# Local attention of the last two layers: another order of rotation, squares and value copies, and a GpSimd that adds all rotated products

## The reference, cut to what matters

```
h = shift_token(x);  q, k, v = split(h @ wqkv, 3)          # 8 heads of 64
q = l2norm(q) * qs;  k = l2norm(k) * ksc
q = q*cos*scale + rotate_half(q)*sin*scale                 # k: the same, divided by scale
sim = q*8 @ k.T   in windows of 64, own and previous window, causal mask
o = softmax(sim) @ v;  x = x + o @ wo
h = layernorm(shift_token(x));  a, g = split(h @ w1 + b1, 2)
x = x + (a * gelu(g)) @ w2 + b2
```

## Time and profile before

| | |
|---|---|
| median of 3 runs | 1512.34 us (1511.67 to 1512.66) |
| profiled execution | 1508.53 us, span 1506.5 us |
| mean granted TensorE clock | 0.957 |
| busy share of the span: PE, DVE, ACT, POOL | 89%, 67%, 53%, 24% |
| the last two layers | from 1078 us to the end of the span |

### The profile page before, as it was taken

The page is one execution under the profiler, slowest core; times in us unless marked ns, Lnnn a source line. Parts: engine busy times, 40 slices in busy tenths (PEclk is TensorE's granted clock), DMA queues, the critical chain, the costliest instruction groups (busy, mean ns, idle before and its releaser), DMA issues.

```text
span 1506.5 us, 23829 instructions
## 1 busy us (share of the span) xinstructions
PE 1333.5 (89%) x9009; PEld 790.8 (52%) x9009; DVE 1013.3 (67%) x2202; ACT 792.7 (53%) x1681; POOL 361.6 (24%) x288
## 2 busy tenths in 40 slices
PE   6999999999999999999589999987279988799886
PEld 4767677776777673333223333333146654366652
DVE  5767767687766856765577667740967775877755
ACT  4544435444444442434136666675169984499851
POOL 0000000011000003335410000000267771477732
PEclk9999999999999999999569999999589999999998
DMA  5000000000000000002023111100200000000000
GB/s 141 1 1 1 1 1 1 1 1 1 1 1 1 0 1 1 1 0 81 29 77 82 46 37 37 36 3 7 57 1 2 2 2 1 1 2 2 2 1 28
DMA packets 23725, 26.03 MB, mean 17 GB/s; under 512 B 5602, under 2 KB 20140, under 8 KB 22316
## 3 DMA queue, kind: packets, MB, share of 16 engines
q1 hardware_dynamic: 23612, 24.51, 5.5%
HBM read 20.11 MB, written 4.39 MB: 16 GB/s over the span
## 4 chain that ended last, share of the span: by engine, by line
PE 64%; ACT 14%; DVE 13%; issue 4%; POOL 2%; DMA 2%; SPq 0%; POOLq 0%; DVEq 0%; ACTq 0%
PE ps L679 13%; PE ps L699 8%; PE ps L714 7%; ACT probsT L2283 6%; PE ps L1051 4%; PE ps L1010 4%; PE ps L1031 3%; DVE negmax L1437 2%; PE ps L888 2%; PE ps L882 2%; PE ps L1182 2%; PE ps L650 2%; ACT v_st L2253 2%; PE ps L1173 2%; PE ps L872 2%
## 5 line engine op out<-in xcount | busy, mean ns | idle before, releaser
L2208 ACT ACTIVATE probsT<-ps 128x512 f32<-128x512 f32 (+1 forms) x304 | 163.6, 576 | 103.7 <-PE ps L1035 91.6
L1437 DVE TENSOR_REDUCE negmax<-ps 128x1 f32<-128x1024 f32 x128 | 150.7, 1219 | 72.5 <-PE ps L699 72.4
L2030 ACT ACTIVATE probs<-ps,negmax 128x1024 f32<-128x1024 f32 x128 | 142.5, 1114 | 80.5 <-DVE negmax L1437 76.5
L2036 ACT COPY probsT<-ps 128x512 f32<-128x512 f32 x128 | 74.8, 584 | 168.2 <-PE ps L714 168.1
L714 PEld LDWEIGHTS ps<-ident,probs 128*128 128x128 f32 x1024 | 114.5, 141 | 66.2 <-issue 44.0
L714 PE MATMUL ps<-ident,probs 128*128 128x128 f32 x1024 | 138.4, 277 | 6.6 <-DVE probsT L1450 3.4
L2360 POOL TENSOR_SCALAR rstd<-mv 128x4 f32<-128x4 f32 (+1 forms) x23 | 5.3, 233 | 578.5 <-DVE mv L1372 578.4
L1010 PE MATMUL ps<-arena 76*128 76x512 bf16 (+3 forms) x384 | 113.6, 355 | 26.4 <-DVE cmax L1705 20.6
L699 PE MATMUL ps<-k_st,q_st 64*128 64x512 f32 x512 | 128.7, 622 | 5.9 <-ACT probs L2030 5.9
L1705 DVE CUSTOM_DVE_ANT_0 k_st<-ps,rel 128x256 f32<-128x256 f32 (+7 forms) x128 | 96.8, 756 | 44.1 <-PE ps L1010 43.2
L1705 DVE CUSTOM_DVE_ANT_0 q_st<-ps,rel 128x256 f32<-128x256 f32 (+7 forms) x128 | 96.7, 756 | 41.9 <-PE ps L1010 41.0
(11 more groups left out here) (245 smaller groups left out, 2565.1 us busy)
## 6 DMA issues: line engine op xcount, KB each, us to landing
arena<-c_parts SPq DMA_DIRECT2D x32, 192.0 KB
arena<-c_parts SPq DMA_DIRECT2D x16, 128.0 KB
arena<-in_L_ffn_w_dram SPq DMA_DIRECT2D x3, 512.0 KB
c_parts<-probsT SPq DMA_DIRECT2D x2, 768.0 KB, 3.5
arena<-in_c_far_dram SPq DMA_DIRECT2D x16, 96.0 KB
c_parts<-work SPq DMA_DIRECT2D x2, 768.0 KB, 11.3
work<-in_L_ffn_wqkv_dram SPq DMA_DIRECT2D x1, 1536.0 KB
x_sb<-in_L_attn_x_dram SPq DMA_DIRECT2D x2, 512.0 KB, 5.9
```

The lines of the kernel that those rows point to most:

```text
L1437: dve.tensor_reduce(negmax[:, u:u + 1], s2, AX_X, ALU.max, negate=True).then_inc(s_a_negmax, 1)
L2030: act.activation(probs[:, u % NPB, :], s2, ACT.Exp, bias=negmax[:, u:u + 1], accum_out=rowsum[:, u:u + 1]).then_inc(s_a_exp, 1)
L2208: act.activation(c_p[:, kt % 2, j0:j0 + heads, q0 - kt * P:q0 - kt * P + n], ps[:, 4 + c % 2, 0:heads * n].rearrange("p (h n) -> p h n", n ...
```

## The change

In both layers: `rotate` no longer waits for the square but for the projection, and the square waits for the rotation. On VectorE the rotation moves from the start of step t (for tile t+2) to the end of step t (for tile t+3), with the inverse of the row sums between its two products; the norms go behind the residual; the copy of 64 rows of values is done there instead of on ScalarE. On ScalarE the square goes from the end of a step to behind the value copies. On GpSimd one addition of 1024 columns (`add_halves`) takes the place of the two halves, at the end of a step and a tile further ahead.

```diff
@@ VectorE
-                    dve.wait_ge(s_d_sq, n + 1)
+                    dve.wait_ge(s_d_qkp, n + 1)
                     if exists(t, -2):
                         dve.wait_ge(s_d_add, n - 1)
                     dve.tensor_tensor(mA, qk, heads(rot_c[:, t:t + 1, :, :]), ALU.mult)
+                    if between:
+                        between()
...
-            def add_keys(l, t):
-                    n, par = TILES * l + t, t % 2
-                    dve.wait_ge(s_d_m, n + 1)
-                    dve.tensor_tensor(d_kq[par][:, INNER:2 * INNER], d_mA[:, par, INNER:2 * INNER],
-                                      d_mB[:, par, INNER:2 * INNER], ALU.add).then_inc(s_d_addk, 1)
...
             def step(l, t, piece=None):
-                    if exists(t, 2):
-                        rotate(l, t + 2)
+                    def inverse():
+                        dve.wait_ge(s_d_e, n + 1)
+                        dve.reciprocal(d_rr[:, par, :], d_sum[:, par, :]).then_inc(s_d_rr, 1)
...
-                    if exists(t, 2):
-                        add_keys(l, t + 2)
-                        norms(l, t + 2)
                     if exists(t, -2):
                         dve.wait_ge(s_d_w, n - 1)
                         z = xT[:, (t - 2) * P:(t - 1) * P]
                         dve.tensor_tensor(z, ps[:, 3, 0:P], z, ALU.add).then_inc(s_d_z, 1)
+                    if exists(t, 2):
+                        norms(l, t + 2)
                     if piece:
                         piece()
+                    if exists(t, 3):
+                        rotate(l, t + 3, inverse)
+                    elif exists(t, 0):
+                        inverse()
                     if exists(t, 0):
-                        dve.wait_ge(s_d_e, n + 1)
-                        dve.reciprocal(d_rr[:, par, :], d_sum[:, par, :]).then_inc(s_d_rr, 1)
+                        if exists(t, -1):
+                            dve.wait_ge(s_d_v, n)
+                            if exists(t, -2):
+                                dve.wait_ge(s_d_o, n - 1)
+                            dve.tensor_copy(d_vs[WIN:P, par, :], d_va[WIN:P, 1 - par, :]).then_inc(s_d_vs, 1)
+                        else:
+                            dve.sem_inc(s_d_vs, 1)
@@ ScalarE
-                    act.wait_ge(s_d_qkp, n + 1)
+                    act.wait_ge(s_d_m, n + 1)
...
+                        act.wait_ge(s_d_vp, n + 1)
                         if exists(t, -1):
-                            act.wait_ge(s_d_v, n)
-                            act.copy(d_vs[WIN:P, par, :], d_va[WIN:P, 1 - par, :])
-                        act.wait_ge(s_d_vp, n + 1)
+                            act.wait_ge(s_d_vs, n)
                         act.copy(d_va[:, par, :], ps[:, 3, :])
                         act.copy(d_vs[0:WIN, par, :], ps[0:WIN, 3, :]).then_inc(s_d_v, 1)
+                    if exists(t, 2):
+                        square(l, t + 2)
...
-                    if exists(t, 3):
-                        square(l, t + 3)
@@ GpSimd
+            def add_halves(l, t):
+                    pool.wait_ge(s_d_m, n + 1)
+                    if exists(t, -2):
+                        pool.wait_ge(s_d_qkt, n - 1)
+                    pool.tensor_tensor(kq, d_mA[:, par, :], d_mB[:, par, :], ALU.add).then_inc(s_d_add, 1)
...
                     if exists(t, 2):
                         unit_norm(l, t + 2)
+                    if exists(t, 3):
+                        add_halves(l, t + 3)
@@ TensorE, before the product with the values
+                        if exists(t, -2):
+                            pe.wait_ge(s_d_vs, n)
```

More of the change, by code:

```diff
@@ L423, in build @@
         s_d_v = sem("s_d_v")
-        s_d_addk = sem("s_d_addk")
+        s_d_vs = sem("s_d_vs")
         s_d_s = sem("s_d_s")
@@ L1765, in tables, with rotate @@
                                                   sc[:, n:n + 1, e:e + 32].to_broadcast([P, QT, 32]), ALU.mult))
-            def rotate(l, t):
+            def rotate(l, t, between=None):
                     n, par = TILES * l + t, t % 2
@@ L1784, in rotate @@
                     ins.then_inc(s_d_m, 1)
[L1786 to L1790 removed]
             def norms(l, t):
                     n, par = TILES * l + t, t % 2
+                    dve.wait_ge(s_d_sq, n + 1)
                     dve.tensor_reduce(ss[:, par, :], d_sq[:, par, :].rearrange("p (h d) -> p h d", d=HD2),
@@ L1884, in _ @@
             rotate(0, 0)
-            add_keys(0, 0)
             norms(0, 0)
             rotate(0, 1)
-            add_keys(0, 1)
             norms(0, 1)
+            rotate(0, 2)
             for l in range(DEPTH):
@@ L1936, in _ @@
                     last_norm(0)
-                else:
-                    add_keys(l + 1, 0)
-                    norms(l + 1, 0)
                 gated(l, 10)
                 if not last:
+                    norms(l + 1, 0)
                     next_shift(l, 1)
@@ L1955, in _ @@
                     add_down(l, 3)
-                    add_keys(l + 1, 1)
                     norms(l + 1, 1)
                     next_shift(l, 2)
+                    rotate(l + 1, 2)
                     next_shift(l, 3)
@@ L2309, in _ @@
                 if l == 0:
-                    for t in range(3):
+                    for t in range(2):
                         square(l, t)
@@ L2330, in _ @@
                     if l + 1 < DEPTH:
-                        if j == 8:
+                        if j == 9:
                             square(l + 1, 0)
@@ L2335, in _ @@
                     act.activation(tpre[:, 1:2], eps_c[:, 0:1], ACT.Exp)
-                    square(l + 1, 2)
         @block.gpsimd
@@ L2478, in _ @@
             pool.wait_ge(s_d_init, 1)
-            def unit_norm(l, t):
+            def add_halves(l, t):
                     n, par = TILES * l + t, t % 2
@@ L2496, in step, with begin @@
                     n, par = TILES * l + t, t % 2
-                    if exists(t, 0):
-                        v = d_p[:, par, :, :]
-                        pool.wait_ge(s_d_rr, n + 1)
-                        pool.tensor_tensor(v, v, d_rr[:, par, :].unsqueeze(2).to_broadcast([P, H2, P]), ALU.mult)\
-                            .then_inc(s_d_p, 1)
+                    v = d_p[:, par, :, :]
+                    pool.wait_ge(s_d_rr, n + 1)
+                    pool.tensor_tensor(v, v, d_rr[:, par, :].unsqueeze(2).to_broadcast([P, H2, P]), ALU.mult)\
+                        .then_inc(s_d_p, 1)
                     if exists(t, 2):
                         unit_norm(l, t + 2)
-            unit_norm(0, 0)
-            unit_norm(0, 1)
+                    if exists(t, 3):
+                        add_halves(l, t + 3)
+            def begin(l):
+                add_halves(l, 0)
+                unit_norm(l, 0)
+                add_halves(l, 1)
+                unit_norm(l, 1)
+                add_halves(l, 2)
+            begin(0)
             for l in range(DEPTH):
@@ L2515, in _ @@
                 if l + 1 < DEPTH:
-                    unit_norm(l + 1, 0)
-                    unit_norm(l + 1, 1)
+                    begin(l + 1)
             for c in range(NCH):
```

8 lines of the change are left out of this document (4 added, 4 removed).

## The result

The changed kernel takes 1522.01 us (median of 4 runs, 1521.3 to 1522.66) against 1512.45 of the kernel before (4 runs, 1511.67 to 1512.66): +9.6 us, ratio 1.007, 95% interval 1.0057 to 1.0082. The forecast was 1522, with 1507 to 1526 as range. The profiled execution took 1521.85 us, its span is 1519.8 (before 1508.53 and 1506.5).

What follows compares the result with a forecast made beforehand. The prediction took a 9.04 us TensorE-ScalarE loop as the bound, replaced by a clamp-held loop of 9.42. Terms 7.6 + 5.6 - 3.6 + 1.1 - 1.3 = +9.4 on 1508.53, plus 3.8 to the median, gave 1522 us (range 1507 to 1526).

Steps and rivals of the forecast that it cites:

- the loop: TensorE and ScalarE chain of a steady step, 9.04 us; without the square 8.14, but a second loop of TensorE allows 8.77.
- the clamp is held: Steady steps: VectorE's clamp waits nearly 2.1 us for GpSimd's addition; step 9.04 to 9.42, +7.6 us over both layers.
- One sign of the forecast: In the profile after, ScalarE should stand idle over 1 us a step waiting for the transposes of q and k.
- the terms above: Forecast parts: steady steps +7.6, step 13 +5.6, layer starts -3.6, first layer's start +1.1, between layers -1.3; sum +9.4 us.
- The locked loop: Steady steps: addition, clamp, product, inverse, multiplication, power, scaling, and addition again, closing at 9.42 us; forecast's chance 0.50.
- the bounds: Limits for GpSimd's addition of 1024 columns: 2.13 us, from an earlier stage's operation, to 2.56, twice the half.
- the addition is always first: Steady steps: addition starts 4.0 after the multiplication, clamp 4.03 to 4.14, so the addition leads by 0.03 to 0.14 us.
- the clamp gets in ahead of the addition: Rival, chance 0.15: order turns, steady steps of some 8.8 and 9.2 alternate, mean about 9.04; 1514 to 1517 us.
- Step 13: Clamp ahead of the shift released 2.0 later, step 12's shift (0.84) in the loop: +2.8 per layer, +5.6 us.
- The first steps: First two steps of each layer are free of the clamp's loop and lose the square: 4 x 0.90 = -3.6 us.
- Step 14: No long addition against the clamp in steps 14 and 15; missing ScalarE copy and waiting copy about cancel: 0.
- The third rotation ahead of the tables: Layer start: it leaves the first maxima's path (2.4), but the third addition holds the tables as long: 0 (-2.3 to +1).

Runs made afterwards that it cites:

- copy on ScalarE: Changed kernel with the copy of the 64 rows of values back on ScalarE, in front of its own tile's values: 1516.49 us, ratio 1.0035.
- second profile: The same changed kernel measured and profiled once more, nothing edited: 1522.95 us, ratio 1.0078 to the kernel before.
- no clamp: Changed kernel without VectorE's clamp of the 16 sums of squares; the power takes the sums as they are: 1511.40 us, ratio 1.0001.
- two additions: Changed kernel with GpSimd's addition of 1024 columns cut into two of 512: 1510.31 us, ratio 1.0000.
- early shift: Changed kernel with the two shift copies of steps 12 and 13 at the start of VectorE's step, ahead of the maxima: 1514.41 us, ratio 1.0019.
- whole addition in the old order: Kernel before, with GpSimd adding both halves in one instruction of 1024 columns and VectorE no keys: 1513.57 us, ratio 1.0020.
- clamp on GpSimd: Changed kernel with the clamp on GpSimd ahead of the power, and the shift of steps 12 and 13 early: 1503.41 us, ratio 0.9945.

## Why the prediction was right, and where its steps were off

**Right: the mechanism.** The forecast was that the square leaves the loop, which is then worth at most 8.77; that the clamp is held to the end of GpSimd's addition and rotation, inverse and multiplication queue behind it; that the copy of values takes about 1 us (median 1.07); and that the shift makes step 13 long. Taking the clamp out gives exactly 8.77, with no other edit. One sign of the forecast did not show: ScalarE waits 0.3 to 0.5 us a step for the transposes of q and k, not over 1; its wait, 0.73 or 1.76, is for the copy of values.

**The number: partly luck.** 1522 was the profile before (1508.53) + 9.4 + 3.8, where 3.8 was the distance of that profile from its median. The changed kernel's profile lies only 0.2 under its median. The forecast for the profile, 1517.9, was 3.9 short of 1521.85: 2.0 of it is the later start of the changed code, 1.9 the terms above. So 3.9 too little and 3.6 too much make up for each other, and within the terms steady steps and step 13 miss in opposite directions. That 1522 came out to the tenth says nothing of the steps.

**The locked loop is there, but longer.** The prediction had 9.42 for a step in which the clamp loses every time. Such steps exist, up to four in a row, and take 9.80. Its addition was put at 2.13, from another operation of that shape (a subtraction); this one takes 2.36, near the middle of the bounds: +0.23. And the power takes 3.10 rather than 2.91: +0.19. Together 9.84, measured 9.80.

**The failed step: that the addition is always first.** The prediction had the addition 4.0 and the clamp 4.03 to 4.14 after the end of the multiplication (its own terms add up to 4.18 at the upper end). The longer power (+0.19) moves the addition to 4.19 (1199.09 to 1203.28); the clamp comes at 4.19 too. This was the rival "the clamp gets in ahead of the addition", with its condition (the copy of values delays the power by 0.1 or more) fulfilled by 0.19. What followed was its pattern, not its steps: 8.77 and 9.59 in place of 8.8 and 9.2, since the addition is longer. That the delayed power alone brings the alternation about is refuted by the copy on ScalarE, where it isn't delayed and the steps are 8.77 and 9.09. Twenty steady steps cost 4.15 in the first profile, not 7.6, and 8.0 in the second, where the clamp loses the tie more often.

**Step 13 was mis-sized.** 12.3 was forecast, 13.98 and 14.04 came (12.79 and 12.73 in the second profile). In layer 1 of the first, TensorE's idle time ahead of its second four transposes grew by 1.6 (2.68 for 1.09), and from there to the mask it took 1.06 more (1235.93 to 1239.24 is 3.31, before 2.25) at a granted clock of 0.58 against 1.00. The remaining 1.8 come from a step whose start is late behind what was held in step 12 (the shift in layer 1, the clamp in layer 2): early in step 13 TensorE waits 1.12, 0.43 and 0.17 us for the multiplication of the probabilities and ScalarE's copies. The clock was not in the forecast at all, and it doesn't fall every time. Four profiles (the changed kernel twice, no clamp, two additions) have eight step 13s with a wait of 2.39 to 2.73 ahead of these transposes. Of these, four have a granted clock of 0.57 to 0.66 behind it and need 3.80 to 4.04 to the mask; the other four have 1.00 and need 2.74. What decides between them no run shows. That the copies' place makes the step long is shown by the early shift.

**The first steps.** -0.90 each was forecast for four. The first step of each layer gave 0.91 and 0.69; the second gave 0.36 and lost 0.91. In it the scaling of the maxima, with two inputs in SBUF, is held by the scaling of the keys, and the clamp by the addition, as at 1117.65 in VectorE's rows, then GpSimd's:

```profile
1117.65 0.89 DVE L1811 SCALAR_TENSOR_TENSOR d_nm<-d_nm,d_rn 128x8 f32<-128x8 f32 x1
...
1117.48 1.04 POOL L2502 TENSOR_TENSOR q_st<-q_st,d_rn 128x512 f32<-128x512 f32 x1
```

Its usual row is 0.17. I had looked for held copies and scalings but not for this one. That these holds are what the second step lost was not tested. Step 14 (+1.7 and -0.35) and the end (-1.3; -1.0 to -1.7 in the other kernels with the new order, but -0.55 with the copy on ScalarE and -0.5 with the whole addition in the old order) were forecast as nothing; no run takes them apart, and they stay open. The third rotation ahead of the tables did what was said: the table product (L1762) takes 2.73 behind it, and nothing is won.

**What holds what.** The Trainium skill, page "SBUF — State Buffer", section "SBUF: two separate sides", says that a VectorE operation in a two-port mode, or one with two SBUF inputs against a GpSimd operation that reads SBUF, and the GpSimd operation shut each other out for the whole instruction. For additions, scalings and multiplications the rows agree: the clamp and the maxima's scaling end 0.02 to 0.04 after GpSimd's instruction, the copies of 512 columns 0.27 to 0.29 after it (1224.32 and 1224.03), which is most of their own 0.42. For the power they don't, as before: the early shift's copies run in 0.42 and 0.43 inside one.

## What to carry to other kernels

A cheap instruction can be the dearest of a step when it shares SBUF with a long one on GpSimd: look at what VectorE starts during each of those and reckon with the rest of that one instruction, then cut it to pieces no longer than the slack behind it (here 1.28 was free and 2.36 was not) or move the starts under instructions that hold nothing. When two starts lie within a tenth of a microsecond by the working, forecast both orders and their mixture. Where a wait leaves TensorE a gap as long as here (2.4 to 2.7 us), work out both cases behind it: with the full clock, and with the lower one, which cost 1.1 to 1.3 us in half of the cases. And before reading a split of costs between stages off one profile, take a second: here the steady steps cost 4.15 in one and 8.0 in the other, at nearly the same time.

## What the runs showed of the hardware that was not expected

- A tie can go either way: with starts in the same hundredth of a microsecond the clamp was held 2.2 once and not at all another time.
- A VectorE copy that waits for GpSimd's multiplication delays the next GpSimd instruction: the power's row is 3.09 to 3.10 behind a waiting copy and 2.91 without one (with the copy on ScalarE). With the clamp on GpSimd in between, the clamp takes 0.43 and the power 2.94.
- The same two-input shape of 1024 columns takes 2.36 as an addition in these rows and 2.13 as a subtraction in an earlier stage; the multiplication takes 1.90, but 2.13 where VectorE's copy starts right beside it (1235.69, with the copy of values at 1235.65).
- Reduce and reciprocal on SBUF data are held in no row seen: the sum of squares at 1119.07 starts inside an addition (1118.48 to 1120.85) with its usual 1.20, the reciprocal at 1205.46 inside another (1203.28 to 1205.67) with its usual 0.20.
- TensorE's clock behind the same wait is not always the same: in step 13 of the changed kernel it was 0.58 and 0.66 after waits of 2.68 in one profile and stayed at 1.00 after 2.73 and 2.68 in the other.
